# VectorE's turns wait for the first gather three quads ahead, and its work inside a turn is reordered

## The chip, the cores and the metric

One core of one Trainium2 chip. The metric is the device time of one execution in microseconds (us); three runs are given, with their median.

## What is computed

Four graph layers on 3125 nodes with 128 features and 53125 edges that are sorted by destination. Only the first one gathers rows by edge, and it is the one that matters here:

```python
# layer 0, h = relu(layernorm(x))
msg_in = concat([h[src], h[dst], edge_attr_2])          # 53125 x 258
msgs   = maximum(msg_in @ mW1 + mb1, 0) @ mW2 + mb2
agg    = segment_sum(msgs, dst) / clip(count(dst), 1)
upd    = maximum(concat([h, agg]) @ uW1 + ub1, 0) @ uW2 + ub2 + h
x      = x + layernorm(upd) * gamma + beta
# layers 1 to 3: layernorm, relu, a sum over each node's edges (plain, with weights
# normed by the weighted degree, normed by the plain degree), dense products, residual
```

## The kernel before

The edges are cut into 104 quads of 512 (four columns of 128). `P = h @ mW1[0:128]` is computed for all nodes and stored to HBM (`p_rows`); for each quad **GpSimd** (POOL) issues four indirect DMAs of 128 rows of `P` into a ring of `GS` = 6 quads (`G`, in the tile `room`), line 816, waiting for the message product of the quad six before. That is its only work from the table's store to the end of the loop over quads (the sweep), apart from seven gathers of edge windows behind quad 2.

**TensorE**, in its iteration q: `pre(q + 1)` adds the gathered rows (lines 1785, against the identity) and the products of the edges' destination rows and attributes (line 1786) in PSUM; `blocks(u, 0)` and `blocks(u, 1)` with u = q - 4 (lines 1816, 1818) build the tables of edge counts and weights that layers 1 to 3 use as dense matrices; `seg(q)` (line 1799) sums a quad's messages by node with a one-hot matrix; `q_window(q + 4)` (line 1772) makes the destination rows; and in 33 iterations (`SLOT`) one step A, U or V of layer 0's node part of a piece of two node tiles follows. **ScalarE** takes the messages' relu (line 956), makes the rows that spread the destinations (962, 969) and reads the blocks (981, 986). **SyncE** loads and stores; among others it stores the degrees (line 641), 16 bytes at a time, and loads them back for the pieces (607, 608).

**VectorE**, in its turn q (`turn_in_step`, from q = 5 on): `add(q - 1)` adds a quad's sums from PSUM to `ST` (line 1289); `mask_operand` and three `weighed_operand` with u = q - 2 (lines 1312, 1321, bf16, both inputs in SBUF), `lo_operand` (line 1325, likewise), `q_window(q + 3)` copies the destination rows from PSUM (line 1296), `onehot(q + 2)` makes four one-hot matrices (line 1302, f32, one SBUF tensor in). Behind a turn stands node work: the degrees of the edges' blocks (`block_degrees`, lines 1371 to 1374, in four turns from 6 to 15), the addition of biases to `h` and `x` (1396, 1401) and the steps of a piece (`piece_steps`: 1193 to 1208, 1424, 1426, 1432). Each engine follows its own program in the order written; semaphores join them. `mask_operand(u)` waits for the blocks of u - 3, that is for the end of TensorE's iteration q - 1; `add` waits for a later product of TensorE.

After the sweep come the dense products of layers 1 to 3, in which TensorE is busy nearly all the time, and the last piece's node steps.

## Time and profile before

| | |
|---|---|
| time, median of 3 runs | 913.08 us (908.39 to 915.04) |
| time of the profiled execution | 912.11 us |
| its span, first to last instruction | 910.3 us |
| mean granted TensorE clock | 0.965 of full speed |
| first gather of the sweep starts, last starts | 27.72 us, 588.96 us |
| busy: TensorE, VectorE, ScalarE, GpSimd | 830.6, 633.4, 504.4, 509.5 us |

The span is 1.8 us shorter than the time of the same execution. A busy share is a mean over stages with different limits: in the last 320.3 us (590.0 to 910.3) TensorE is busy for 311.1 us, in the sweep (27.7 to 590.0) for 505.7 of 562.3 us, while GpSimd is busy for 433.6 us of the sweep.

### The profile page before, as it was taken

How to read it: one execution, taken by the hardware profiler on the slowest of the kernel's cores; microseconds unless marked ns; L12 is line 12 of the kernel's file. 1: busy time of each engine (PE TensorE's matmuls, PEld its weight loads, DVE VectorE, ACT ScalarE, POOL GpSimd, SP SyncE). 2: the span in 40 equal slices, each digit the busy share in tenths (PEclk: the TensorE clock that was granted, in tenths of full speed). 3: DMA queues.
4: the chain of work that ended last, by engine and by line, in shares of the span. 5: the costliest groups of instructions: out<-in, count | busy, mean ns of one | idle time of the engine just before them, and what ended most of it. 6: DMA issues, size and time to landing. Idle time of an engine off the chain costs nothing.

```text
span 910.3 us, 18961 instructions
## 1 busy us (share of the span) xinstructions
PE 830.6 (91%) x6949; PEld 774.1 (85%) x6949; DVE 633.4 (70%) x1769; ACT 504.4 (55%) x1005; POOL 509.5 (56%) x496
## 2 busy tenths in 40 slices
PE   4539878699999989999999998999999999999996
PEld 4439878699899989999998998978899888898886
DVE  7449999678799996998887988648741311127663
ACT  4226656477587776877777877734353011115874
POOL 8577777777777777777777777771210000014110
PEclk9669989899999999999999999999999999999999
DMA  6534546666756655566555665582148777686501
GB/s 176 163 85 128 163 144 177 131 205 204 223 169 189 203 171 157 181 178 206 180 173 166 191 183 178 156 270 73 46 181 327 295 294 293 237 289 204 152 24 29
DMA packets 104976, 163.68 MB, mean 180 GB/s; under 512 B 14698, under 2 KB 65425, under 8 KB 104878
## 3 DMA queue, kind: packets, MB, share of 16 engines
q1 hardware_dynamic: 91230, 134.19, 44.5%
q0 software_dynamic: 13648, 28.21, 12.2%
q8 instruction: 59, 0.97, 0.4%
q14 instruction: 39, 0.32, 0.1%
HBM read 107.92 MB, written 54.43 MB: 178 GB/s over the span
## 4 chain that ended last, share of the span: by engine, by line
POOL 41%; PE 38%; issue 13%; DVE 4%; DMA 3%; ACT 1%; SPq 0%; DVEq 0%; POOLq 0%
POOL room L816 40%; PE ps L1960 15%; PE ps L1945 14%; PE ps L1929 2%; DMA room<-p_rows,idx 2%; PE ps L1785 2%; PE ps L1786 1%; PE ps L1799 1%; PE ps L1721 1%; PE ps L1818 1%; PE ps L1816 1%; POOL pair L816 1%; DMA x<-in_x 1%; PE ps L1824 1%; DMA rest<-degrees 0%
## 5 line engine op out<-in xcount | busy, mean ns | idle before, releaser
L816 POOL DMA_INDIRECT room<-p_rows,idx x416 | 426.9, 1026 | 132.2 <-issue 125.0
L1785 PE MATMUL ps<-room,ident 128*128 128x128 f32 x832 | 174.8, 293 | 40.5 <-DMA room<-p_rows,idx 39.6
L1785 PEld LDWEIGHTS ps<-room,ident 128*128 128x128 f32 x832 | 131.6, 199 | 44.8 <-DMA room<-p_rows,idx 35.3
L1786 PE MATMUL ps<-room 128*128 128x128 f32 x832 | 166.6, 283 | 0.0
L1321 DVE TENSOR_TENSOR room<-room,Wp 128x800 bf16<-128x800 bf16 x294 | 158.9, 569 | 3.4
L1816 PE MATMUL ps<-room 128*128 128x200 bf16 x784 | 158.2, 254 | 2.3 <-ACT room L986 2.3
L1818 PE MATMUL ps<-room 128*128 128x100 bf16 x1568 | 157.9, 208 | 0.0
L1818 PEld LDWEIGHTS ps<-room 128*128 128x128 bf16 x1568 | 145.0, 98 | 3.8
L1960 PE MATMUL ps<-room,h 128*128 128x256 f32 (+1 forms) x650 | 133.5, 367 | 0.0
L1786 PEld LDWEIGHTS ps<-room 128*128 128x128 f32 x832 | 132.1, 200 | 0.0
L1960 PEld LDWEIGHTS ps<-room,h 128*128 128x128 f32 x650 | 117.7, 190 | 13.9
L956 ACT ACTIVATE g<-ps 128x512 f32<-128x512 f32 x104 | 62.2, 598 | 113.2 <-PE ps L1786 113.2
L981 ACT ACTIVATE room<-ps 128x400 uint8<-128x400 f32 x196 | 98.4, 502 | 35.5 <-PE ps L1818 30.8
L1799 PE MATMUL ps<-g 128*128 128x128 f32 x832 | 116.8, 284 | 1.1 <-DVE room L1296 1.0
L1945 PE MATMUL ps<-wide_room,parts 128*128 128x512 f32 (+2 forms) x520 | 108.4, 363 | 0.0
L1799 PEld LDWEIGHTS ps<-g 128*128 128x128 f32 x832 | 101.9, 193 | 1.3 <-issue 1.2
L1302 DVE TENSOR_SCALAR g<-iota,dstT 128x128 f32<-128x128 f32 x416 | 100.9, 317 | 0.0
L1945 PEld LDWEIGHTS ps<-wide_room,parts 128*128 128x128 f32 x520 | 88.9, 188 | 14.1
L986 ACT ACTIVATE room<-ps 128x400 f32<-128x400 f32 x196 | 99.1, 506 | 0.0
L962 ACT ACTIVATE room<-room,npio 125x512 bf16<-125x512 bf16 x104 | 75.8, 729 | 23.4 <-DMA room<-dst_row 23.4
L909 ACT ACTIVATE sd<-mv,eps 128x2 f32<-128x2 f32 (+3 forms) x45 | 13.3, 295 | 130.3 <-DVE mv L1196 130.2
L1816 PEld LDWEIGHTS ps<-room 128*128 128x128 bf16 x784 | 77.2, 99 | 6.4 <-issue 3.7
(195 smaller groups left out, 1074.0 us busy)
## 6 DMA issues: line engine op xcount, KB each, us to landing
weight_blocks<-room SPq DMA_DIRECT2D x49, 800.0 KB
room<-weight_blocks SPq DMA_DIRECT2D x11, 3200.0 KB
room<-dst_row SPq DMA_DIRECT2D x52, 256.0 KB
count_blocks<-room SPq DMA_DIRECT2D x49, 200.0 KB
room<-count_blocks SPq DMA_DIRECT2D x6, 1600.0 KB
room<-p_rows,idx POOLq DMA_INDIRECT x416
first_c<-count_blocks SPq DMA_DIRECT2D x4, 1600.0 KB, 11.2
room<-weight_blocks SPq DMA_DIRECT2D x2, 2000.0 KB
```

Of the source, the lines that this page charges most:

```text
L816: return pool.indirect_dma_start(to, None, table, bass.IndirectOffsetOnAxis(ap=at, axis=axis))
L981: act.activation(cnt_out[:, u % OUTS, :, at16].rearrange("p h (b w) -> p b h w", w=4), of, ACT.Copy)\
L986: act.activation(w_out[:, u % OUTS, :, at16].rearrange("p h (b w) -> p b h w", w=4), of, ACT.Copy)\
L1302: last = dve.tensor_scalar(oh[:, q % OS, c, :], iota[:, :], dstT[:, q, c:c + 1], None, ALU.is_equal)
L1321: dve.tensor_tensor(mov[:, k, 1 + a, :, :, :], mov[:, k, 0, :, :, :], blocks_of(Wp[:, a, :], u, KCOLS), ALU.mult)
L1785: pe.matmul(to, ident[:, :], G[:, n % GS, c, :], start=True, stop=False)
L1786: last = pe.matmul(to, sT[:, n % TS, 128 * c:128 * c + 128], Qr[:, n % QS, :], start=False, stop=True)
L1799: last = pe.matmul(bank(2 + n % 2, 128), R[:, n % RS, c, :], oh[:, n % OS, c, :], start=c == 0, stop=c == 3)
L1816: pe.matmul(to.rearrange("p (a c) -> p a c", a=2), lo, mov[:, k, 0:2, i, :, t], start=True, stop=False)
L1818: weighed = pe.matmul(to[:, KCOLS:2 * KCOLS], lo, mov[:, k, 1 + a, i, :, t], start=False, stop=a == PARTS - 1)
L1945: last = pe.matmul(to, Hr[:, t, a, :], at[:, k, 0:n], start=a == 0 and t == 0, stop=a == 1 and t == NT - 1)
L1960: last = pe.matmul(bank(dense_bank(j))[:, at:at + 32 * c], h[:, t, :], ring_w[(2 * j + half) % 3][:, 0:c, t, :], start=t == 0, stop=t == N ...
```

## The change

Five edits. (1) An indirect DMA of the sweep also increments a new semaphore `s_issued` when GpSimd has issued it (`engine_sem`), and each turn of VectorE from q = 5 to q = 100 begins with a wait for 4(q + 3) + 1 of them: the first gather of quad q + 3. (2) Inside a turn the four one-hot products are spread (one before the mask, one behind the first weighed operand, two ahead of `lo_operand`), and the Q copy stands behind all three weighed operands, where it stood behind the first. (3) The node work of a turn stands behind the Q copy, ahead of the last two one-hots and `lo_operand`, where it stood at the turn's end. (4) The degrees, four times four instructions in turns 6, 9, 12 and 15, go into sixteen turns, 5 to 20, one instruction each; the factors into turn 21 (before 17); SyncE stores them at q = 22 (before 20), and still loads them back at q = 23. (5) The biases of `h` and `x`, in every other turn from 10 and from 35, now alternate from turn 22 and from turn 23.

```diff
--- before.py
+++ after.py
@@ -63,9 +63,9 @@
     PW = 256
     BEGIN = 27
     APART = 7
-    BIAS_H, BIAS_X = 10, 35
-    DEGREES = 6
-    assert BIAS_H + 2 * NPC <= BIAS_X and BIAS_X <= BEGIN + 9
+    DEGREES = 5
+    BIAS_H, BIAS_X = DEGREES + 17, DEGREES + 18
+    assert BIAS_X <= BEGIN + 5
 
     def complete(t):
 
@@ -363,6 +363,7 @@
         s_Qmm = sem("q_window_in_psum")
         s_Qr = sem("q_window_ready")
         s_pre = sem("messages_in_psum")
+        s_issued = sem("gathers_issued")
         s_R = sem("messages_ready")
         s_seg = sem("quad_in_psum")
         s_add = sem("quad_added")
@@ -635,7 +636,7 @@
                     sp.wait_ge(s_pre, q + 1)
                     sp.wait_ge(s_sT, q + 1)
                     rows_of_two(q - 1 + TS)
-                if q == BEGIN - 7:
+                if q == BEGIN - 5:
                     sp.wait_ge(s_deg, 4)
                     for k in range(4):
                         sp.dma_start(deg_tab[k, :].rearrange("(g p w) -> p g w", g=GROUPS, w=4), degw[:, k, :, :])\
@@ -812,8 +813,9 @@
             pool.wait_ge(s_w, 48)
             pool.tensor_copy(pw[:, :, 1], w_l).then_inc(s_pk, 1)
 
-            def rows_at(to, table, at, axis=0):
-                return pool.indirect_dma_start(to, None, table, bass.IndirectOffsetOnAxis(ap=at, axis=axis))
+            def rows_at(to, table, at, axis=0, issued=None):
+                return pool.indirect_dma_start(to, None, table, bass.IndirectOffsetOnAxis(ap=at, axis=axis),
+                                               engine_sem=issued)
 
             edge_at = win_tab.rearrange("a (b c) -> (a b) c", c=256)
             pool.wait_ge(s_edE, 1)
@@ -822,7 +824,7 @@
                 if q >= GS:
                     pool.wait_ge(s_pre, q - GS + 1)
                 for c in range(4):
-                    rows_at(G[:, q % GS, c, :], P_tab, idx[:, q, c:c + 1]).then_inc(s_gat[q % GS], 16)
+                    rows_at(G[:, q % GS, c, :], P_tab, idx[:, q, c:c + 1], 0, s_issued).then_inc(s_gat[q % GS], 16)
                 if q == 2:
                     pool.wait_ge(s_pst, 48)
                     pool.wait_ge(s_sidx, 1)
@@ -1295,12 +1297,13 @@
                     dve.wait_ge(s_pre, n - QS + 1)
                 dve.tensor_copy(Qr[0:WIN, n % QS, :], q_bank(n)[0:WIN, :]).then_inc(s_Qr, 1)
 
-            def onehot(q):
-                if q >= OS:
+            def onehot(q, columns=range(4)):
+                if q >= OS and 0 in columns:
                     dve.wait_ge(s_seg, q - OS + 1)
-                for c in range(4):
+                for c in columns:
                     last = dve.tensor_scalar(oh[:, q % OS, c, :], iota[:, :], dstT[:, q, c:c + 1], None, ALU.is_equal)
-                last.then_inc(s_oh, 1)
+                if 3 in columns:
+                    last.then_inc(s_oh, 1)
 
             def blocks_of(a, u, n):
                 return a[:, CB * u:CB * u + CB].rearrange("p (i a t) -> p i a t", a=1, t=2)\
@@ -1366,13 +1369,16 @@
                 link(dve.tensor_scalar(whole1[:, 3:4], whole1[:, 1:2], 0.0, None, ALU.is_equal))
                 dve.tensor_tensor(flag_i[:, :], whole1[:, 2:3], whole1[:, 3:4], ALU.mult).then_inc(s_flag, 1)
 
-            def block_degrees(w):
-                dve.wait_ge(s_kmm, 3)
-                link(dve.tensor_scalar(T_b, Dd, float(w), None, ALU.is_equal))
-                dve.tensor_reduce(degw[:, 0, :, w], by_block(T_b), AX.X, ALU.add)
-                link(dve.tensor_tensor(by_block(T_c), by_block(T_b), win[:, :, :, 1], ALU.mult))
-                last = dve.tensor_reduce(degw[:, 1, :, w], by_block(T_c), AX.X, ALU.add)
-                link(last)
+            def degree_step(w, k):
+                if k == 0:
+                    dve.wait_ge(s_kmm, 3)
+                    link(dve.tensor_scalar(T_b, Dd, float(w), None, ALU.is_equal))
+                elif k == 1:
+                    link(dve.tensor_reduce(degw[:, 0, :, w], by_block(T_b), AX.X, ALU.add))
+                elif k == 2:
+                    link(dve.tensor_tensor(by_block(T_c), by_block(T_b), win[:, :, :, 1], ALU.mult))
+                else:
+                    link(dve.tensor_reduce(degw[:, 1, :, w], by_block(T_c), AX.X, ALU.add))
 
             def block_factors():
                 dve.tensor_scalar(degw[:, 3, :, :], degw[:, 0, :, :], 1.0, None, ALU.min).then_inc(s_deg, 1)
@@ -1451,21 +1457,41 @@
 
             for n in range(LEAD):
                 q_window(n)
+            def node_work(q):
+                if DEGREES <= q < DEGREES + 16:
+                    degree_step((q - DEGREES) // 4, (q - DEGREES) % 4)
+                if q == DEGREES + 16:
+                    block_factors()
+                if BIAS_H <= q < BIAS_H + 2 * NPC and (q - BIAS_H) % 2 == 0:
+                    bias_h0_piece((q - BIAS_H) // 2)
+                if BIAS_X <= q < BIAS_X + 2 * NPC and (q - BIAS_X) % 2 == 0:
+                    bias_x_piece((q - BIAS_X) // 2)
+                if q == BIAS_X + 2 * NPC:
+                    link(dve.tensor_tensor(bc[:, B_L1, :], bc[:, B_L1, :], bc[:, B_L1B, :], ALU.add))
+                piece_steps(q)
+
             def turn_in_step(q):
                 u = q + 2 - LAG
+                if 4 * (q + 3) + 1 <= 4 * NQ:
+                    dve.wait_ge(s_issued, 4 * (q + 3) + 1)
                 add(q - 1)
                 if SLOT.get(q - 1, " ")[0] == "A":
                     read_A_piece(SLOT[q - 1][1], slot_bank(q - 1))
+                if q + 2 < NQ:
+                    onehot(q + 2, (0,))
                 if u < STEPS:
                     mask_operand(u)
                     weighed_operand(u, 0)
-                if q - 1 + LEAD < NQ:
-                    q_window(q - 1 + LEAD)
+                if q + 2 < NQ:
+                    onehot(q + 2, (1,))
                 if u < STEPS:
                     weighed_operand(u, 1)
                     weighed_operand(u, 2)
+                if q - 1 + LEAD < NQ:
+                    q_window(q - 1 + LEAD)
+                node_work(q)
                 if q + 2 < NQ:
-                    onehot(q + 2)
+                    onehot(q + 2, (2, 3))
                 if u < STEPS:
                     lo_operand(u)
 
@@ -1486,17 +1512,6 @@
                         onehot(q + 2)
                 else:
                     turn_in_step(q)
-                if DEGREES <= q < DEGREES + 12 and (q - DEGREES) % 3 == 0:
-                    block_degrees((q - DEGREES) // 3)
-                if q == DEGREES + 11:
-                    block_factors()
-                if BIAS_H <= q < BIAS_H + 2 * NPC and (q - BIAS_H) % 2 == 0:
-                    bias_h0_piece((q - BIAS_H) // 2)
-                if BIAS_X <= q < BIAS_X + 2 * NPC and (q - BIAS_X) % 2 == 0:
-                    bias_x_piece((q - BIAS_X) // 2)
-                if q == BIAS_X + 2 * NPC:
-                    link(dve.tensor_tensor(bc[:, B_L1, :], bc[:, B_L1, :], bc[:, B_L1B, :], ALU.add))
-                piece_steps(q)
             add(NQ - 1)
 
             def factors_begin(r):
```

## Rows read from the trace of the kernel before

**Rows 1.** The page, the chain of work that ended last: by engine, by line.

```profile
POOL 41%; PE 38%; issue 13%; DVE 4%; DMA 3%; ACT 1%; SPq 0%; DVEq 0%; POOLq 0%
POOL room L816 40%; PE ps L1960 15%; PE ps L1945 14%; PE ps L1929 2%; DMA room<-p_rows,idx 2%; PE ps L1785 2%; PE ps L1786 1%; PE ps L1799 1%; PE ps L1721 1%; PE ps L1818 1%; PE ps L1816 1%; POOL pair L816 1%; DMA x<-in_x 1%; PE ps L1824 1%; DMA rest<-degrees 0%
```

**Rows 2.** The waits: engine, line, releaser: us in total, times, longest.

```profile
POOL room L816 <- issue: 125.0, 410, 0.3
...
POOL room L816 <- PE ps L1786: 1.2, 4, 0.3
```

**Rows 3.** Line 816 alone: duration ns min/median/max, first and last start us.

```profile
L816 POOL DMA_INDIRECT room<-p_rows,idx x416: 941/948/1822, 27.7 to 589.0; - x139
```

**Rows 4.** The page, costliest groups: GpSimd's gathers.

```profile
L816 POOL DMA_INDIRECT room<-p_rows,idx x416 | 426.9, 1026 | 132.2 <-issue 125.0
```

**Rows 5.** Timeline of TensorE: message products begin (us, duration, line).

```profile
242.70 0.45 PE L1785 MATMUL ps<-room,ident 128*128 128x128 f32 x2
...
311.26 0.45 PE L1785 MATMUL ps<-room,ident 128*128 128x128 f32 x2
```

**Rows 6.** Timeline of GpSimd and VectorE about a long gather at 298 us.

```profile
298.03 1.26 POOL L816 DMA_INDIRECT room<-p_rows,idx  x1 [0.30 <-issue]
...
297.90 0.57 DVE L1321 TENSOR_TENSOR room<-room,Wp 128x800 bf16<-128x800 bf16 x1
```

**Rows 7.** The same about one at 435 us.

```profile
435.08 1.35 POOL L816 DMA_INDIRECT room<-p_rows,idx  x1 [0.30 <-issue]
...
434.59 0.68 DVE L1325 TENSOR_TENSOR room<-iota_l,LOt 128x1024 bf16<-128x1024 bf16 x1
435.19 0.41 DVE L1424 TENSOR_TENSOR h<-h,bc 128x256 f32<-128x256 f32 x1
```

**Rows 8.** The same in turn 12, with a block of degrees.

```profile
123.67 1.55 POOL L816 DMA_INDIRECT room<-p_rows,idx  x1 [0.30 <-issue]
125.52 1.82 POOL L816 DMA_INDIRECT room<-p_rows,idx  x1 [0.30 <-issue]
...
123.79 0.61 DVE L1371 TENSOR_SCALAR pair<-pair 128x896 f32<-128x896 f32 x1
124.43 1.09 DVE L1372 TENSOR_REDUCE degw<-pair 128x7 f32<-128x896 f32 x1
125.44 1.08 DVE L1373 TENSOR_TENSOR pair<-pair 128x896 f32<-128x896 f32 x1
```

**Rows 9.** Line 816 by stretches: columns us, GpSimd busy (instructions), clock, DMA.

```profile
69.00:152.40 83.40, 65.72 (x59) 0.96 0.50 147
...
445.50:590.00 144.50, 110.84 (x111) 1.00 0.57 177
```

**Rows 10.** Timeline of VectorE, turn 75, and the gather that opens quad 78.

```profile
451.75 0.29 DVE L1289 TENSOR_TENSOR ST<-ST,ps 128x128 f32<-128x128 f32 x1 [0.63 <-PE ps L1845]
452.47 0.57 DVE L1312 TENSOR_TENSOR room<-iota_k,Kt 128x800 bf16<-128x800 bf16 x1 [0.43 <-PE ps L1818]
453.08 0.57 DVE L1321 TENSOR_TENSOR room<-room,Wp 128x800 bf16<-128x800 bf16 x1
453.57 0.28 DVE L1296 COPY room<-ps 125x128 f32<-125x128 f32 x1
453.77 1.05 DVE L1321 TENSOR_TENSOR room<-room,Wp 128x800 bf16<-128x800 bf16 x2
454.74 1.03 DVE L1302 TENSOR_SCALAR g<-iota,dstT 128x128 f32<-128x128 f32 x4
455.54 0.68 DVE L1325 TENSOR_TENSOR room<-iota_l,LOt 128x1024 bf16<-128x1024 bf16 x1
...
454.77 0.95 POOL L816 DMA_INDIRECT room<-p_rows,idx  x1 [0.30 <-issue]
```

**Rows 11.** Timeline of SyncE and TensorE about the degrees' stores.

```profile
164.91 3.92 SPq L641 DMA_DIRECT2D degrees<-degw  x4
...
179.26 0.80 PE L1785 MATMUL ps<-room,ident 128*128 128x128 f32 x2 [6.89 <-DMA room<-p_rows,idx]
```

**Rows 12.** Timeline of GpSimd: a gather of quad 23, and the sweep's last.

```profile
169.02 0.94 POOL L816 DMA_INDIRECT room<-p_rows,idx  x1 [0.30 <-issue]
...
588.96 0.94 POOL L816 DMA_INDIRECT room<-p_rows,idx  x1 [0.31 <-issue]
```

## The prediction

> **What bounds the kernel now.** I read the chain of waits first. It runs 40% of its length through line 816, GpSimd's gathers, and 13% through "issue", time in which an engine waits for nothing; the dense products follow [rows 1]. The table of waits says the same from GpSimd's side: 0.30 us ahead of nearly every gather with no releaser, and only 1.2 us in all for TensorE [rows 2]. So the ring of six quads never holds GpSimd back: from 27.7 us, its first gather, to the last, which starts at 588.96 and takes 0.94 (589.9), it issues without a pause [rows 3, 12]. The other engines must follow, and what it saves there ends the sweep earlier. Behind 589.9 come 320.4 us of the 910.3 span, which the change doesn't touch.
>
> **TensorE** is no far second. Where it runs behind the gathers, so that they don't hold it, pre(35) starts at 242.70 and pre(49) at 311.26: 68.6 us for 14 quads, 4.90 us each [rows 5]. Four gathers at their least cost 4 x (0.945 + 0.305) = 5.00. GpSimd stays the bound even without any excess, by a tenth.
>
> **The excess.** The shortest gather takes 0.941, half of them at most 0.948, the longest 1.822 [rows 3]; the mean is 1.026 [rows 4]. Against 0.945, 416 gathers have 416 x 0.081 = 34 us of excess. That is all that can be gained. Where it comes from is seen by laying the two timelines on each other. A gather from 298.03 took 1.26: a tensor_tensor with both inputs in SBUF had begun 0.13 before it and ended at 298.47; the gather lasted 0.82 past that end [rows 6]. Since a plain one takes 0.945, its sensitive instant is about 0.13 after its start: an operation of that kind which began before the gather and covers the instant delays it to its own end. The one at 435.08 took 1.35: line 1325 ended at 435.27, past the instant, but line 1424 had already begun at 435.19, and the gather waited for that too (435.60 + 0.82 = 436.42, seen 436.43) [rows 7]. An operation that begins behind the gather costs nothing, and the one-hots little: four from 454.74 on leave a gather at 0.95 [rows 10].
>
> **The change, part by part.**
>
> *Degrees.* Now one block is four instructions in a row. Line 1371 stands behind 1325 and the gather takes 1.55 (excess 0.61), 1373 makes the next one 1.82 (excess 0.87) [rows 8]. There are four of the second kind and three of the first: 4 x 0.87 + 3 x 0.61 = 5.3 us. Afterwards each instruction stands alone behind the Q copy, which reads PSUM. At a random place an operation of length d covers the instant, having begun in time, with d - 0.18 of the 1.25 us between gathers, and costs half of that on average: for 1.08 us 0.9/1.25 x 0.45 = 0.32, for 0.61 about 0.08. Four of each: 1.6. **Gain 3.7 us.** Bounds: 5.3 if none is hit, -0.2 if all are, 4 x 0.87 + 4 x 0.5 = 5.5.
>
> *Node work behind the Q copy.* Twenty gathers show the pattern of rows 7, 1.34 to 1.36 us, 0.40 excess each: 8 us. Without the second operation 1325 alone would leave about 0.07 there (its end lies 0.19 behind the gather's start [rows 7]); 20 x 0.33 = 6.6 is freed. Given back: some 57 node operations of 0.41 us (24 biases, 33 of pieces) at random places cost 0.23/1.25 x 0.12 = 0.02 each, about 1.3; and 1325, now behind the node work, loses the place where it costs 0.07: at random 0.5/1.25 x 0.25 = 0.10, and in turns with 0.41 of node work nearer 0.25, about 3 us more over 96 turns. **Gain 2.5 us**, from 6.6 down to -3.
>
> *The wait.* In 65 of the 96 turns from 5 to 100 VectorE starts ahead of what it will wait for; turn 75 began at 451.75, the gather ended at 455.72, 3.97 later [rows 10]. Mean over the 65: 2.9 us. Queued behind it: add(q - 1), the operands u = q - 2, the Q copy of q + 3, the one-hots of q + 2. TensorE needs these late: the operands two iterations on, the one-hots two, the Q copy before seg(q + 1). Turn 75 shows the steps: 0.61 from mask to weighed, 0.49 per weighed, 0.20 per one-hot, add and copy, 0.60 for 1325: 3.87 us, against 5.0 or more for four gathers, so the turn still fits. The mask at 452.47 marks the end of TensorE's iteration 74; at 4.90 each, iteration 76 begins near 457.3, 1.6 us behind the gather in question, and reaches seg about half an iteration later, at 4.1 to 4.3 (an estimate); the Q copy, now at 2.8 to 3.0, comes 1.2 or so earlier. I cost the wait on TensorE at nothing, covered by that; were it gone, a quad's tenth of slack would go first, and then the six quads of ring cover it.
>
> What the wait does to the gathers: it fixes the phase. With the gather's end at 0 and an estimated 0.1 for the semaphore, the next instants are at 0.43, 1.68, 2.93, 4.18, and the turn is add 0.1, one-hot 0.3, mask 0.5 to 1.07, weighed 1.1 to 1.67, one-hot 1.6, weighed 1.8 to 2.36 and 2.3 to 2.85, copy 2.77, one-hots 2.97, 3.17, line 1325 3.36 to 4.04. No long operation covers an instant, but the second comes within 0.01 us. Excess per turn now: in the last stretch 110.84 - 111 x 0.945 = 5.9 us over 28 quads, 0.21 [rows 9] (in the stretch with the degrees 10.0 over 59 gathers, 0.68 a quad). With the phase exact it would fall to some 0.07 (node work of 0.41 pushes 1325 over 4.18 in about half the turns). With the phase 0.1 to 0.4 late, a weighed operand covers 1.68 each turn: 0.1 to 0.39. The trace shows no wait of VectorE on GpSimd in the sweep and no such post, so both ends stay; I take **nothing**, between -9 and +16 us (65 x 0.14, 65 x 0.24).
>
> *The degrees' stores* of 16-byte pieces (3.92 us to issue) slow the gathers' landing: TensorE began pre(23) at 179.26, the gather having ended at 169.96, and had stood 6.89 us [rows 11, 12]. They move two quads on and SyncE's loads at q = 23 now wait for them, with the next row loads behind. TensorE loses about the same 7 us two quads later. GpSimd doesn't feel it: the ring gives 25 us. Cost nothing; if the stall doubled it would still fit.
>
> *Biases in alternate turns*: the same instructions, priced above; V needs its bias ten turns later.
>
> **Sum.** 3.7 + 2.5 = 6.2 us. 912.1 - 6.2 = 905.9, forecast **906 us**; the profiled execution lies 1.0 below the median of the three runs, within their spread of 6.6.
>
> The Trainium skill, "SBUF — State Buffer", section "Who interferes with whom", says that tensor_tensor takes only the read side of the pair shared with GpSimd and that descriptor generation needs the write side, so that it doesn't hold up such DMAs; 2-port operations like the one-hots do, for the whole instruction. Rows 6 and 7 speak against it. It would leave only the three 0.61 of line 1371 to gain.
>
> **Rivals.**
>
> *Only line 1371 matters.* The long gathers beside tensor_tensor would be coincidence: 912.1 - 1.8 = 910. Against it: the ends agree within 0.01 us in rows 6 and 7 and in 20 more. With it I count that the gains are eaten by other hits, since the order is new: 909 to 914. Chance 0.20.
>
> *The phase fits*: 65 turns lose another 0.14: 906 - 9 = **897**. For: no operation over an instant in the list above. Against: a margin of 0.01, node work in most turns. Chance 0.20.
>
> *The phase is bad* (slower): the post is seen 0.2 to 0.4 us later than I assume, for instance at the end of the 0.30 us between gathers, and the first weighed operand covers the second instant in every waiting turn. 65 x 0.24 = 16 more, 906 + 16 = **922**. It decides from about 0.05 us of lateness on, and outweighs the 6.2 once the mean hit is above 0.1 a turn. For: the delay isn't in this trace. Chance 0.10.
>
> *The post costs GpSimd time.* 416 gathers at 0.02 us each are 8 us: 914. Nothing in the trace shows it. 0.05.
>
> **Numbers.** Forecast 903 to 910, chance 0.45; the rivals as above. The range 896 to 918 leaves out the better part of the bad phase and the tail of the good one. One per cent, 9 us, is about what a measurement of this kernel can tell from no change. Faster by more (below 904): the good phase and a fifth of the forecast's case, 0.30. Slower by more (above 922): 0.06. Within: 0.64.
>
> **What would show it.** Right: the last gather ends near 584; mean of line 816 near 1.011; no gather of 1.5 or more but for two or three; the 1.35 group gone; a new wait of VectorE on GpSimd, some 3 us in 50 to 65 turns; TensorE's stall at pre(25) in place of pre(23). Wrong: the last gather near 589.9 with long gathers at a fixed place of the turn; gaps between gathers above 0.30 us; TensorE waiting at seg for the Q copy; or a time behind the last gather other than 320 us.

## The result, and the profile after

The median after is **905.29 us** (9 runs, 903.87 to 908.8), against 912.84 (9 runs, 908.39 to 916.15) for the kernel before on the same chip: ratio 0.9919, interval 0.9898 to 0.9941. The profiled execution took 905.0 us, its span is 903.1. The forecast was 906.

The page of the kernel after, its chain of waits, which answers to [rows 1]:

```profile
PE 46%; POOL 36%; issue 11%; DMA 3%; DVE 3%; ACT 1%; SPq 0%; DVEq 0%; POOLq 0%
POOL room L817 35%; PE ps L1975 15%; PE ps L1960 14%; PE ps L1800 3%; DMA room<-p_rows,idx 3%; PE ps L1801 3%; PE ps L1814 2%; PE ps L1944 2%; PE ps L1831 2%; PE ps L1833 2%; PE ps L1736 1%; POOL pair L817 1%; DMA x<-in_x 1%; PE ps L1787 1%; POOL h L801 0%
```

GpSimd and "issue" fell from 54% to 47% of the chain, and TensorE's message products (lines 1800 and 1801) came in for them: the two engines are close enough that the chain now changes hands within the sweep. The gathers keep the largest part of it. The page's group, [rows 4] after:

```profile
L817 POOL DMA_INDIRECT room<-p_rows,idx x416 | 419.5, 1008 | 132.5 <-issue 122.5
```

The same line alone (ns min/median/max, first and last start), [rows 3] after:

```profile
L817 POOL DMA_INDIRECT room<-p_rows,idx x416: 940/944/1823, 27.8 to 581.6; - x139
```

The gathers are busy for 419.5 us instead of 426.9. I call *excess* what lies above 416 x 0.945 = 393.1: 26.4 us after, 33.8 before. It fell by 7.4, the last gather ends at 582.5 instead of 589.9, also 7.4 earlier, and 903.1 - 582.5 = 320.6 us follow it, as before (320.4). The whole gain is excess that went away.

The waits (us in total, times, longest), which answer to [rows 2], with VectorE's first step of a turn:

```profile
POOL room L817 <- issue: 122.5, 402, 0.3
...
POOL room L817 <- PE ps L1801: 3.7, 12, 0.3
...
DVE ST L1291 <- DMA room<-p_rows,idx: 60.5, 69, 1.0
```

The new wait is the last row: 69 turns, 0.9 us each, at most 1.0. GpSimd's pause between gathers is 0.30 as before, and TensorE's part in it has the same length: it is the name of the last releaser that changed, not a delay. Line 817 by stretches, with the columns of [rows 9]:

```profile
69.00:151.50 82.50, 63.59 (x63) 0.98 0.54 164
442.60:582.50 139.90, 107.30 (x108) 0.99 0.58 179
```

In the first stretch, with the degrees, the excess is 63.59 - 63 x 0.945 = 4.1 us over 63 gathers, where it was 10.0 over 59. In the second it is 107.30 - 108 x 0.945 = 5.2, 0.19 a quad, where it was 0.21. So **the gain lies nearly all in the degrees' stretch**: counted by quads, the gathers of quads 8 to 22 had 9.6 us of excess and have 2.9, which is 6.7 of the 7.4. In the late stretch the five edits together brought almost nothing. The timeline says why. VectorE's turn 74, and the gathers beside it (the first one opens quad 77):

```profile
443.01 0.29 DVE L1291 TENSOR_TENSOR ST<-ST,ps 128x128 f32<-128x128 f32 x1 [1.02 <-DMA room<-p_rows,idx]
443.21 0.32 DVE L1304 TENSOR_SCALAR g<-iota,dstT 128x128 f32<-128x128 f32 x1
443.46 0.56 DVE L1315 TENSOR_TENSOR room<-iota_k,Kt 128x800 bf16<-128x800 bf16 x1
444.05 0.58 DVE L1324 TENSOR_TENSOR room<-room,Wp 128x800 bf16<-128x800 bf16 x1
444.55 0.28 DVE L1304 TENSOR_SCALAR g<-iota,dstT 128x128 f32<-128x128 f32 x1
444.74 1.05 DVE L1324 TENSOR_TENSOR room<-room,Wp 128x800 bf16<-128x800 bf16 x2
445.71 0.28 DVE L1298 COPY room<-ps 125x128 f32<-125x128 f32 x1
445.91 0.41 DVE L1438 TENSOR_TENSOR parts<-h,parts 128x256 fp32r<-128x256 f32 x1
446.25 0.52 DVE L1304 TENSOR_SCALAR g<-iota,dstT 128x128 f32<-128x128 f32 x2
446.64 0.68 DVE L1328 TENSOR_TENSOR room<-iota_l,LOt 128x1024 bf16<-128x1024 bf16 x1
448.17 0.29 DVE L1291 TENSOR_TENSOR ST<-ST,ps 128x128 f32<-128x128 f32 x1 [0.85 <-DMA room<-p_rows,idx]
...
442.03 0.94 POOL L817 DMA_INDIRECT room<-p_rows,idx  x1 [0.30 <-PE ps L1801]
443.28 0.94 POOL L817 DMA_INDIRECT room<-p_rows,idx  x1 [0.30 <-issue]
444.52 0.95 POOL L817 DMA_INDIRECT room<-p_rows,idx  x1 [0.30 <-issue]
445.77 0.94 POOL L817 DMA_INDIRECT room<-p_rows,idx  x1 [0.30 <-issue]
447.02 1.12 POOL L817 DMA_INDIRECT room<-p_rows,idx  x1 [0.30 <-issue]
```

The gather ends at 442.97 and the turn begins at 443.01, 0.04 later; the next gather of a quad (447.02) releases turn 75 in the same way. Three gathers pass undisturbed: the long operations beside them begin behind their starts, or end at most 0.11 behind them (the weighed operand of 444.05). Then the node operation of 0.41 (line 1438) has pushed `lo_operand` (line 1328) to 446.64: it begins 0.38 ahead of the gather that opens the next quad and ends at 447.32, and that gather lasts to 448.14, 0.82 past it. Turn 75 begins at 448.17, so it is late by the same 0.17 as the gather that it waits for, and the phase is kept.

To sort the excess I put each gather that starts behind 80 us and lasts over 0.965 down to the VectorE operation whose end, plus 0.82, fits its end best. After: line 1328 66 gathers with 16.4 us (46 of them 0.12 to 0.20 each, 17 near 0.49), the weighed operands (line 1324) 25 with 6.0 us. Of these, 11 stand in turns that also read a piece's A, which puts them later, and 13 in turns that VectorE reached late, with no idle time ahead of `add` (turns 37, 44 and so on). No gather is put down to the node work or the degrees any more. Before: `lo_operand` 2.1 us, weighed operands 7.7, the mask 2.5, the one-hots 1.9, the degrees 5.3, node operations chained behind `lo_operand` 9.5. So the node work and the degrees freed some 15 us, and `lo_operand`, pushed by them over the next quad's gather, took 14 back. The phase is fixed, and one operation still misses it.

### The profile page after: what moved, and what is told of

It reads as the page before. It is cut to its first block, busy times and chain, and to the rows that moved or that the text cites. A ratio compares the mean times of both kernels' runs of the same rounds, so it can differ in the third digit from the quotient of the medians.

```text
span 903.1 us, 18961 instructions
## 1 busy us (share of the span) xinstructions
PE 829.3 (92%) x6949; PEld 772.3 (86%) x6949; DVE 627.9 (70%) x1769; ACT 502.9 (56%) x1005; POOL 501.6 (56%) x496
## 4 chain that ended last, share of the span: by engine, by line
PE 46%; POOL 36%; issue 11%; DMA 3%; DVE 3%; ACT 1%; SPq 0%; DVEq 0%; POOLq 0%
POOL room L817 35%; PE ps L1975 15%; PE ps L1960 14%; PE ps L1800 3%; DMA room<-p_rows,idx 3%; PE ps L1801 3%; PE ps L1814 2%; PE ps L1944 2%; PE ps L1831 2%; PE ps L1833 2%; PE ps L1736 1%; POOL pair L817 1%; DMA x<-in_x 1%; PE ps L1787 1%; POOL h L801 0%
## 5 line engine op out<-in xcount | busy, mean ns | idle before, releaser
L817 POOL DMA_INDIRECT room<-p_rows,idx x416 | 419.5, 1008 | 132.5 <-issue 122.5
L1800 PE MATMUL ps<-room,ident 128*128 128x128 f32 x832 | 173.1, 291 | 39.7 <-DMA room<-p_rows,idx 37.4
L1833 PEld LDWEIGHTS ps<-room 128*128 128x128 bf16 x1568 | 143.9, 97 | 3.5
L983 ACT ACTIVATE room<-ps 128x400 uint8<-128x400 f32 x196 | 98.4, 502 | 25.5 <-PE ps L1833 24.6
L1304 DVE TENSOR_SCALAR g<-iota,dstT 128x128 f32<-128x128 f32 x416 | 111.5, 293 | 0.6
L1291 DVE TENSOR_TENSOR ST<-ST,ps 128x128 f32<-128x128 f32 x104 | 29.7, 286 | 80.5 <-DMA room<-p_rows,idx 60.5
```

The costliest lines, as they stand in the source:

```text
L817: return pool.indirect_dma_start(to, None, table, bass.IndirectOffsetOnAxis(ap=at, axis=axis), engine_sem=issued)
L983: act.activation(cnt_out[:, u % OUTS, :, at16].rearrange("p h (b w) -> p b h w", w=4), of, ACT.Copy)\
L1304: last = dve.tensor_scalar(oh[:, q % OS, c, :], iota[:, :], dstT[:, q, c:c + 1], None, ALU.is_equal)
L1800: pe.matmul(to, ident[:, :], G[:, n % GS, c, :], start=True, stop=False)
L1833: weighed = pe.matmul(to[:, KCOLS:2 * KCOLS], lo, mov[:, k, 1 + a, i, :, t], start=False, stop=a == PARTS - 1)
```

## The experiments

Each ratio is taken against runs of the kernel before on the same chip as the experiment; their medians were 912.84 for the kernel after, 912.74 for e1 to e4, 915.46 for e5 to e8 and 912.45 for e9 to e12. *Excess* is line 816's or 817's busy time minus 393.1 us, from the profiled execution, one for each kernel. The times of one kernel spread by 2 to 9 us, so a difference of 2 or 3 us of excess between two kernels is not shown by it alone.

| kernel | median us | ratio, interval | excess us | last gather ends |
|---|---|---|---|---|
| before | 912.84 | 1 | 33.8 | 589.9 |
| after | 905.29 | 0.9919, 0.9898 to 0.9941 | 26.4 | 582.5 |
| e1_no_wait | 919.74 | 1.0061, 1.0038 to 1.0085 | 39.7 | 596.6 |
| e2_wait_only | 925.40 | 1.0136, 1.0104 to 1.0168 | 45.4 | 601.8 |
| e3_degrees_only | 913.27 | 0.9998, 0.9977 to 1.0019 | 34.2 | 590.1 |
| e4_lo_first | 893.02 | 0.9788, 0.9757 to 0.9818 | 14.6 | 570.5 |
| e5_old_places | 907.78 | 0.9934, 0.9905 to 0.9962 | 29.4 | 585.3 |
| e6_mask_early | 955.82 | 1.0448, 1.0407 to 1.0489 | 77.4 | 633.7 |
| e7_lo_first_no_wait | 903.28 | 0.9879, 0.9831 to 0.9927 | 22.1 | 577.8 |
| e8_order_only | 938.77 | 1.0264, 1.0224 to 1.0304 | 60.8 | 616.4 |
| e9_fitted | 896.37 | 0.9806, 0.9769 to 0.9843 | 16.3 | 572.2 |
| e10_wait_later | 906.95 | 0.9924, 0.9895 to 0.9954 | 26.6 | 582.5 |
| e11_pairs_apart | 912.69 | 1.0004, 0.9979 to 1.0028 | 31.7 | 587.3 |
| e12_wait_fitted | 907.46 | 0.9942, 0.9922 to 0.9961 | 28.1 | 583.6 |

The end of the last gather less the excess is between 555.5 and 556.9 us in all fourteen; the span behind it differs between 320.4 and 324.7 us from one profiled execution to another, though no edit touches it.

### The wait alone: e1 and e2

Theory: the wait fixes the place of VectorE's long operations between the gathers, and its worth depends on the order inside the turn. Rival: the wait is worth nothing, and the gain comes from the degrees and the node work (the prediction's own sum). e1 takes it out of the kernel after, e2 puts it into the kernel before; both keep the new increment by GpSimd.

```diff
# e1, in after (e2 adds these lines, and engine_sem=s_issued on the gathers, to before)
-                if 4 * (q + 3) + 1 <= 4 * NQ:
-                    dve.wait_ge(s_issued, 4 * (q + 3) + 1)
```

> The changed kernel without VectorE's wait; GpSimd still posts. Theory (the wait fixes the phase at +0.03 us and only moves the hits; the gain is in the degrees' turns and in the pairs that are taken apart): 905 to 908, gathers' excess 26 to 30 us. Rival (the wait carries the gain: without it the spread operations hit at random, 0.36 us a quad from quad 38 on): 911 to 915, excess 34 us or more.

> The kernel before with the post and the wait alone, its order kept. Theory (a fixed phase is good or bad by the order: here the mask would start at about +0.24 us, 0.07 before the second gather, and cover its sensitive instant in every waiting turn, 0.37 us each): slower than before, 918 to 928, with a group of gathers near 1.3 us. Rival (waiting in itself keeps VectorE out of GpSimd's way): 905 to 911. Rival (the post or the wait costs nothing and brings nothing): 912.

Without the wait the excess is 39.7: the other four edits **cost** 5.9 us, and the wait brings 39.7 - 26.4 = 13.3. Added to the old order it costs 45.4 - 33.8 = 11.6. The same wait has both signs, so its worth is that of the order behind it. The forecast for e1 (905 to 908) missed, for it gave the wait no part in the gain, and its rival (911 to 915) had the direction and not the size. The forecast for e2 (918 to 928) held. The timeline of e2 shows the bad fit, in VectorE's turn and the two gathers about it:

```profile
312.48 0.29 DVE L1291 TENSOR_TENSOR ST<-ST,ps 128x128 f32<-128x128 f32 x1 [1.03 <-DMA room<-p_rows,idx]
312.68 0.57 DVE L1314 TENSOR_TENSOR room<-iota_k,Kt 128x800 bf16<-128x800 bf16 x1
...
311.51 0.94 POOL L817 DMA_INDIRECT room<-p_rows,idx  x1 [0.30 <-issue]
312.75 1.32 POOL L817 DMA_INDIRECT room<-p_rows,idx  x1 [0.30 <-issue]
```

No one-hot stands ahead of the mask here, and it begins 0.07 before the second gather instead of behind it. It ends at 313.25, the gather at 314.07, again 0.82 later. By the sorting above 68 gathers are held so, for 24.6 us.

### The order, without and with the wait: e8 and e6

The prediction never priced edit (2) for itself. e8 has the new order alone, on the kernel before, with node work and degrees at the turn's end and no wait. e6 keeps the wait and moves one thing in the kernel after: the first one-hot goes behind the first weighed operand, so that the mask begins 0.24 earlier.

```diff
# e8, in before
+                if q + 2 < NQ:
+                    onehot(q + 2, (0,))
                 if u < STEPS:
                     mask_operand(u)
                     weighed_operand(u, 0)
-                if q - 1 + LEAD < NQ:
-                    q_window(q - 1 + LEAD)
+                if q + 2 < NQ:
+                    onehot(q + 2, (1,))
                 if u < STEPS:
                     weighed_operand(u, 1)
                     weighed_operand(u, 2)
+                if q - 1 + LEAD < NQ:
+                    q_window(q - 1 + LEAD)
                 if q + 2 < NQ:
-                    onehot(q + 2)
+                    onehot(q + 2, (2, 3))
```

```diff
# e6, in after
-                if q + 2 < NQ:
-                    onehot(q + 2, (0,))
                 if u < STEPS:
                     mask_operand(u)
                     weighed_operand(u, 0)
                 if q + 2 < NQ:
-                    onehot(q + 2, (1,))
+                    onehot(q + 2, (0, 1))
```

> The kernel before with the new order inside a turn alone (one-hots spread, Q copy behind the weighed operands); node work, degrees and biases as before, no wait. Theory (without the wait the operations meet the gathers at random, 0.36 us a quad worked out from their lengths, where the old order's four one-hots in a row had left 0.2): 915 to 921, as the changed kernel without its wait. Rival (the slowness without the wait came from the node work's place ahead of lo_operand): 911 to 914.

> The changed kernel with the first one-hot of a turn moved behind the first weighed operand, so that the mask starts 0.2 us earlier, at about +0.23 us of the turn, 0.07 ahead of the gather whose instant it then covers. Theory (phase is all): every waiting turn pays about 0.36 us more, 75 to 80 turns, 27 us: 925 to 935, with some 80 gathers near 1.31 us. Rival (the gain of the wait is that VectorE's operations are kept back from GpSimd in general, whatever stands first): within 3 us of the changed kernel, 902 to 908.

e8 has 60.8 us of excess, 27.0 more than before, and 2.6% more time. Its forecast, 915 to 921, missed: it took the operations to meet the gathers at random. They don't. `lo_operand` begins 0.12 or 0.13 ahead of a gather in 55 of the 96 turns and hits it each time; before, it began 0.48 or 0.49 ahead in 48 turns, and closer than 0.4 in one. Its timeline:

```profile
399.43 0.58 DVE L1313 TENSOR_TENSOR room<-iota_k,Kt 128x800 bf16<-128x800 bf16 x1 [0.24 <-PE ps L1823]
...
402.29 0.69 DVE L1326 TENSOR_TENSOR room<-iota_l,LOt 128x1024 bf16<-128x1024 bf16 x1
...
399.76 1.07 POOL L816 DMA_INDIRECT room<-p_rows,idx  x1 [0.31 <-issue]
...
402.42 1.37 POOL L816 DMA_INDIRECT room<-p_rows,idx  x1 [0.30 <-issue]
```

The mask ends at 400.01, the gather at 400.83; line 1326 ends at 402.98, the gather at 403.79. The second one is held by 0.42, though the operation began only 0.13 ahead of it. By the sorting, `lo_operand` costs 14.8 us here (2.1 before) and the node operations chained behind it 19.9 (9.5 before).

What ties VectorE to the gathers without a wait can be seen too, and the prediction had no such effect. A one-hot that begins 0.50 to 0.61 behind the start of an ordinary gather is itself held, as here in e8:

```profile
529.61 0.41 DVE L1302 TENSOR_SCALAR g<-iota,dstT 128x128 f32<-128x128 f32 x1
...
529.03 0.94 POOL L816 DMA_INDIRECT room<-p_rows,idx  x1 [0.30 <-issue]
```

It takes 0.41 where 0.28 is usual, and ends at 530.02, 0.05 behind the gather's end; 294 of 296 one-hots so placed in the fourteen traces are held in this way. What follows a held one-hot stands at a fixed place behind the gather's start. That this is what decides where `lo_operand` falls is likely, but no run takes it away.

e6 is the strongest single test, one cheap instruction of VectorE moved by a place:

```profile
472.76 0.29 DVE L1291 TENSOR_TENSOR ST<-ST,ps 128x128 f32<-128x128 f32 x1 [1.37 <-DMA room<-p_rows,idx]
472.96 0.57 DVE L1315 TENSOR_TENSOR room<-iota_k,Kt 128x800 bf16<-128x800 bf16 x1
...
474.45 1.05 DVE L1324 TENSOR_TENSOR room<-room,Wp 128x800 bf16<-128x800 bf16 x2
...
471.78 0.95 POOL L817 DMA_INDIRECT room<-p_rows,idx  x1 [0.30 <-issue]
473.03 1.32 POOL L817 DMA_INDIRECT room<-p_rows,idx  x1 [0.30 <-issue]
474.65 1.67 POOL L817 DMA_INDIRECT room<-p_rows,idx  x1 [0.30 <-issue]
```

The mask holds the second gather for 0.37, in 77 turns (28.4 us; forecast 27, and 925 to 935 in time). That shifts the third gather, so that the pair of weighed operands, begun 0.20 ahead of it, holds it too: the second of them ends near 475.5, and 475.5 + 0.82 is the gather's end (474.65 + 1.67 = 476.32). Line 1324 is charged with 107 gathers and 24.6 us, where the kernel after has 25 and 6.0. Excess 77.4, time +4.5%, with not one instruction more. The first-order price was right (0.36 a turn), the chain behind it was more than the price itself.

### The phase moved by a whole gather: e10

```diff
-                if 4 * (q + 3) + 1 <= 4 * NQ:
-                    dve.wait_ge(s_issued, 4 * (q + 3) + 1)
+                if 4 * (q + 3) + 2 <= 4 * NQ:
+                    dve.wait_ge(s_issued, 4 * (q + 3) + 2)
```

> The changed kernel, waiting for the second gather of the quad instead of the first: the same phase against the gathers, 1.25 us later against TensorE. Theory (the wait costs TensorE nothing as long as the Q copy comes before seg): the Q copy now at 4.1 to 4.3 us is about level with seg, so TensorE is a little late each quad but GpSimd still sets the end; gathers' busy time 418 to 423 us, time 904 to 908. Rival (the prediction's cover of 1.2 us is the true limit, and beyond it each quad pays): 910 or more, TensorE waiting for line 1298 in most iterations.

Excess 26.6 and the ratio 0.9924: a wait one gather, 1.25 us, later changes nothing, since the place between two gathers is the same. TensorE begins to feel it, in the waits of the product that reads the Q copy:

```profile
PE ps L1814 <- DVE room L1298: 2.9, 5, 1.1
```

In the kernel after this row reads 1.0 us, once. So the Q copy's margin is about one gather, as the prediction had it (1.2 us), and the ring covers 2.9 us.

### The other edits by themselves: e3, e5 and e11

e3 has only the degrees' sixteen steps (with their factors in turn 21 and their store two quads later) on the kernel before. e5 is the kernel after with degrees, factors, biases and SyncE's store back in their old turns. e11 is the kernel before with the node work ahead of `lo_operand`, so that no node operation stands right behind it.

```diff
# e3, in before (with degree_step as in after, and SyncE's store at BEGIN - 5)
-                if DEGREES <= q < DEGREES + 12 and (q - DEGREES) % 3 == 0:
-                    block_degrees((q - DEGREES) // 3)
+                if DEGREES <= q < DEGREES + 16:
+                    degree_step((q - DEGREES) // 4, (q - DEGREES) % 4)
```

```diff
# e5, in after (and the reverse of e3)
-    DEGREES = 5
-    BIAS_H, BIAS_X = DEGREES + 17, DEGREES + 18
+    BIAS_H, BIAS_X = 10, 35
+    DEGREES = 6
```

```diff
# e11, in before (node_work holds what stood at the turn's end)
                 if q + 2 < NQ:
                     onehot(q + 2)
+                node_work(q)
                 if u < STEPS:
                     lo_operand(u)
```

> The kernel before with only the degrees in sixteen steps at the turn's end, and SyncE's store two quads later. Theory (the block costs 5.3 us of excess because line 1371 stands behind line 1325 and line 1373 is met every time; alone each is met less often, but 1371 and now also 1373 can stand behind 1325): 2 to 4 us gained, 909 to 911, quads 8 to 22 at 5 to 8 us of excess for 9.6 before. Rival (the moved steps alone explain the gain): 905 to 907, excess of those quads 3 us as in the changed kernel.

> The changed kernel with degrees and biases back in their old turns (one block of four degree instructions each third turn, biases from turns 10 and 35), the wait, the order and the node work's place kept. Theory now (the wait together with an order that fits it carries the gain; the degrees' spreading matters only because it lets turns fit the phase): 907 to 910, the excess of quads 8 to 22 at 5 to 7 us for 2.9 in the changed kernel, the rest equal. Rival (where the degrees stand doesn't matter, as the run with them alone suggests): 905.

> The kernel before, its node work moved ahead of lo_operand and behind the four one-hots, all else as before, no wait. The prediction's term (twenty pairs of line 1325 and an f32 product, 0.40 us each, freed, and some 4 us given back): 2 to 3 us less, 909 to 911, no group near 1.35 us. Rival (without a fixed phase an order can't be priced by the hits it had, the free run settles on others): anything from 912 to 925.

e3: in quads 8 to 22 the excess falls from 9.6 to 8.7, and behind quad 52 it is 13.6 where it was 11.2, though nothing differs there but the moment at which it begins. Alone the edit is worth nothing, where 909 to 911 was forecast: the steps still stand behind `lo_operand`, and the sorting puts 5.1 us down to them, as to the blocks before (5.3). e5: 29.4 against 26.4, 3.0 us of excess for the degrees and biases once the wait is there; the two ratios, 0.9934 and 0.9919, are too close to show it in time. e11: 2.1 us less excess than before, and a ratio of 1.0004, where 909 to 911 was forecast; `lo_operand` alone is now charged with 11.1 us. But its quads 8 to 22 have 5.3 us where they had 9.6, and the degrees, in their old blocks and without a wait, take 0.9 us instead of 5.3. In kernels without the wait, an edit takes its hits away and the next operations, now elsewhere, make others.

### The fit made better: e4, e7, e9 and e12

If line 1328 is late by the node work, it should stand ahead of it. e4 puts `lo_operand` right behind the Q copy; e7 is the same without the wait. e9 adds to e4 what the list of hits asks for next: in turns that read an A the first one-hot stands behind the first weighed operand, and the node work between the third and the fourth. e12 is e2 with one one-hot ahead of the mask.

```diff
# e4, in after (e7 takes the wait out of e4)
+                if u < STEPS:
+                    lo_operand(u)
                 node_work(q)
                 if q + 2 < NQ:
                     onehot(q + 2, (2, 3))
-                if u < STEPS:
-                    lo_operand(u)
```

```diff
# e9, in e4
-                if q + 2 < NQ:
+                if q + 2 < NQ and not reads_A:
                     onehot(q + 2, (0,))
...
-                    onehot(q + 2, (1,))
+                    onehot(q + 2, (0, 1) if reads_A else (1,))
...
+                if q + 2 < NQ:
+                    onehot(q + 2, (2,))
                 node_work(q)
                 if q + 2 < NQ:
-                    onehot(q + 2, (2, 3))
+                    onehot(q + 2, (3,))
```

```diff
# e12, in e2
+                if q + 2 < NQ:
+                    onehot(q + 2, (0,))
                 if u < STEPS:
                     mask_operand(u)
...
-                    onehot(q + 2)
+                    onehot(q + 2, (1, 2, 3))
```

> The changed kernel with lo_operand directly behind the Q copy, ahead of the node work and the last two one-hots. Theory (what is left of the excess is line 1328 pushed by node work over the instant of the gather that opens the next quad, 0.17 or 0.49 us in two turns of three): it then ends at about 3.7 us of the turn, ahead of that instant; excess 26 to about 14 us, the last gather ends near 570, time 893 to 897. Rival (TensorE, at 4.90 us a quad, takes over as the bound): the same fall of excess but 898 to 903, with GpSimd waiting for the ring or the sweep ending well behind the last gather.

> The kernel with lo_operand directly behind the Q copy, without the wait. Theory (the order is good only at a fixed phase): 912 to 920, excess 30 to 40 us for 14.6 with the wait. Rival (this order is better at any phase, since node work no longer pushes the longest operation about): 900 to 908.

> The best version so far (lo_operand directly behind the Q copy, with the wait), its two left groups of hits taken away: in turns that read an A piece no one-hot stands ahead of the mask, so that the first weighed operand ends at about 1.75 us instead of 1.88, and the node work stands between the third and the fourth one-hot, so that a piece's second product starts behind the gather that opens the next quad. Theory (phase alone): 3 to 5 us less excess than 13.9, time 888 to 891. Rival (TensorE at 4.90 us a quad, or the landing, bounds now): 892 to 894 with the last gather earlier but the sweep's end in place.

> The kernel before with the wait and one one-hot moved ahead of the mask, so that the mask starts at 0.43 us and not at 0.24; degrees, biases, node work and the Q copy in their old places. Theory (the phase decides, and the wait alone was slow only because the mask covered the second gather's instant): the 24.6 us of mask hits go, most of the weighed operands' 5.1 with them; gathers' busy time 438.5 to about 408 to 413, time 895 to 900. Rival (the new places of the node work and the Q copy are needed too): 905 or more.

**e4 is the best kernel of the study**, 893.02 us, ratio 0.9788 (0.9757 to 0.9818), within what the theory gave. Its page and its timeline:

```profile
L817 POOL DMA_INDIRECT room<-p_rows,idx x416 | 407.7, 980 | 131.8 <-issue 121.6
```

```profile
432.34 0.68 DVE L1328 TENSOR_TENSOR room<-iota_l,LOt 128x1024 bf16<-128x1024 bf16 x1
432.94 0.47 DVE L1304 TENSOR_SCALAR g<-iota,dstT 128x128 f32<-128x128 f32 x2
434.44 0.29 DVE L1291 TENSOR_TENSOR ST<-ST,ps 128x128 f32<-128x128 f32 x1 [1.02 <-DMA room<-p_rows,idx]
...
432.21 0.95 POOL L817 DMA_INDIRECT room<-p_rows,idx  x1 [0.30 <-issue]
433.46 0.94 POOL L817 DMA_INDIRECT room<-p_rows,idx  x1 [0.30 <-issue]
434.71 0.94 POOL L817 DMA_INDIRECT room<-p_rows,idx  x1 [0.30 <-issue]
```

Line 1328 begins 0.13 behind a gather's start and ends 0.44 before the next: it holds nobody. What is left is 14.6 us, of it 5.3 at weighed operands in 31 turns. Without the wait the same order has 22.1 (e7), where the theory, that this order is good only at a fixed phase, had 30 to 40 and 912 to 920; its rival, an order better at any phase (900 to 908), held. The order is worth 39.7 - 22.1 = 17.6 us without the wait, the wait another 7.5.

e9 missed its forecast (888 to 891) and is no better than e4: 16.3 of excess, the weighed operands still at 35 gathers for 6.1 us; what holds them in those turns isn't the one-hot alone, and stays open. e12 missed its forecast. The mask's hits are gone as meant, but the node work, behind `lo_operand` there, begins some 0.08 ahead of the next quad's gather: 37 hits of biases and pieces of mostly 0.21 each (8.3 us), eight of a degrees' comparison or product (5.1), and eight of `lo_operand` itself (3.6), which begins 0.08 ahead of a gather in seven of them. The weighed operands didn't fall either (6.7 us). I had counted only the operation that I moved.

## Why the prediction was right, step by step

The time and the sign were right, and so was the mechanism, an operation of VectorE over an instant of each gather; how the sum divides among the edits was not. That it came so near is in part luck.

**What bounds the kernel: right.** The last gather moved by 7.4 us and the time by 912.84 - 905.29 = 7.5. In fourteen kernels the last gather's end follows the excess. GpSimd never waited for the ring; 320.6 us stand behind its last gather.

**The instant, 0.13 behind a gather's start, and the tail of 0.82: right**, and shown by moving operations about it (e2, e4, e6). Behind 80 us the fourteen traces have 2027 gathers of over 0.965, and all but 4 end within 0.03 of an operation's end plus 0.82. So the Trainium skill's sentence in "SBUF — State Buffer", section "Who interferes with whom", that tensor_tensor takes only the read side and leaves descriptor generation alone, doesn't hold for these gathers: e6 differs from the kernel after by 51 us of excess through one moved one-hot, and the sorting puts all but some 0.2 us of it down to tensor_tensor operations. Its other half, that tensor_reduce doesn't contend, agrees: in e5 the reductions of the degrees cover the instant of four gathers, from 0.4 ahead to 0.6 behind their starts, and these took 0.94 or 0.95.

**The wait, "I take nothing": wrong, this is the step that failed.** It is worth 13.3 us of excess in this order, 13.0 by the ratios of the medians. I had set it at nothing, between -9 and +16, reckoned on the hits that the old order had. But the order changes with it: the new order running free costs 27.0 (e8), the new places of node work, degrees and biases take 60.8 - 39.7 = 21.1 of it back (e8 against e1), and the wait the last 13.3: 27.0 - 21.1 - 13.3 = -7.4. By the ratios of the medians, in us of 912.8, the three steps are +24.1, -18.5 and -13.0. In this order of adding them, the sum of 6.2 came near 7.4 because what it left out was +27 in one term and about -28 in the others.

**Edit (2), the spread one-hots and the later Q copy, had no term at all**, and is the largest one. I used it only for the list of instants under the wait. That list was right to 0.1 us: behind the gather's end the mask came at 0.49, the weighed operands at 1.08 and 1.77, the copy at 2.74 (0.5, 1.1, 1.8 and 2.77 foreseen), and line 1328 at 3.67 in a turn with 0.41 of node work, where 3.36 stood for one without. The good phase failed at the place that I named, node work pushing that line over the fourth instant. I reckoned 0.07 of excess a quad; it is 0.19 in the last stretch, 66 gathers are hit behind 80 us, and the hits of 0.49, where more node work stands ahead, were not in the 0.07.

**Degrees, 3.7 gained: right in sign, too small, and mostly for another reason.** By the sorting they cost 5.3 us before and nothing after, and quads 8 to 22 lost 6.7. What frees them is the place ahead of `lo_operand`, not the spreading nor the wait: spread but behind it they cost 5.1 (e3), in blocks behind it with the wait 5.1 (e12), in blocks ahead of it 0.9 without the wait (e11) and 1.1 with it (e5). The spreading and the biases' new turns together are the 3.0 between e5 and after.

**Node work behind the Q copy, 2.5 (its own terms give 6.6 - 1.3 - 3 = 2.3): both halves too small.** The sorting has 9.5 us at node operations before and none after, where 6.6 was to be freed and 1.3 to remain; `lo_operand` took back 14.3, where I had 3. I had placed it at random against the gathers, and e8 and the kernel before show that it isn't. In the old order, parted from `lo_operand`, the node work takes 2.1 us of excess and no time (e11). In the new order it is part of the 21.1, which no run divides; the sorting has 25.0 us at node work and degrees in e8 and 1.8 in e1. The rival that the gains are eaten by other hits is what happens in e3 and e11.

**The bad phase** (the rival on the slower side) had the right mechanism and too low a price. The post is seen 0.04 behind the gather's end, earlier than the 0.1 assumed, so it didn't come about. e2 and e6 bring it about, an operation over the second instant in each waiting turn: +11.6 and +51.0 us, where I had 16. In e6 each held gather carries the next one into another operation.

**The post costs GpSimd nothing: right**, 0.30 between gathers as before.

**The wait costs TensorE nothing: right** (e10 finds the end of the margin). Its length I misread: "some 3 us in 50 to 65 turns" was the lead that free turns had gathered. Once each turn waits, it starts a quad behind the last one, and only 60.5 / 69 = 0.9 is left.

**The degrees' stores: right in place, over-priced.** SyncE and TensorE, as in [rows 11]:

```profile
168.09 7.83 SPq L642 DMA_DIRECT2D degrees<-degw  x4
```

```profile
179.49 0.49 PE L1800 MATMUL ps<-room,ident 128*128 128x128 f32 x2 [2.96 <-DMA room<-p_rows,idx]
```

The stores take twice as long to issue (7.83 against 3.92), yet the stall, at pre(25) as forecast, is 2.96 us instead of 6.89. GpSimd feels neither.

**What I said would show it:** last gather 582.5 (584 foreseen), mean 1.008 (1.011), one gather of 1.5 or more, 1.823 (two or three). The group of 1.35 is down to five gathers, three of them ahead of 80 us, but one of about 1.43, from line 1328, took its place.

What no run settles: what fixes VectorE's place against the gathers without the wait, why the span behind the last gather differs by up to 4 us between profiled executions, and which of the remaining weighed operands' hits in e4 could be had.

## What to carry to other kernels

When one engine bounds a stage by many short, evenly spaced instructions and another one disturbs it only at an instant of each, fix the phase between them with a wait that costs nobody, and then choose the order inside the period so that each long operation begins just behind an instant. Price the order and the wait as one edit: the same wait was worth -13.3 us on one order and +11.6 on another, and the hits counted in one order don't tell where they fall once anything is moved. Nor is a place "random" because no semaphore fixes it: before pricing by chance, list where an operation begins against the other engine's instructions, turn by turn. After fitting one operation look at all that follow it in the turn, optional work above all; that is what undid e12 and most of the good phase here.

## What the runs showed of the hardware that I had not expected

- An indirect gather's issue is held by a tensor_tensor with both inputs in SBUF even when that began only 0.07 us ahead of it (e2, e6), and lasts 0.82 us past the operation's end in bf16 (e2) and in f32 ([rows 8]: 125.44 + 1.08 + 0.82 = 127.34, the gather's end) alike; one that begins behind its start costs nothing, even if it covers most of it (e4: line 1328, begun 0.13 behind, the gather took 0.95).
- A semaphore incremented at issue by GpSimd released VectorE 0.04 us behind the end of the gather's record (442.97 to 443.01), without lengthening the 0.30 us between gathers.
- The disturbance goes both ways. A one-hot (tensor_scalar, f32) begun 0.50 to 0.61 behind a gather's start took 0.38 or more in place of 0.28 and ended about 0.99 behind that start (294 of 296 in the fourteen traces). And a one-hot that ends 0.16 to 0.21 behind the start holds the gather to its own end + 0.82, at 0.96 to 1.03 (159 of 160; the other one took 1.45).
- One held gather can hold the following ones: in e6 the mask holds 77 gathers for 28.4 us, and the excess is up by 51.0.
